# A decoder layer on one core: weight preparation in column blocks, bias rows turned on TensorE

## The reference

```python
qkv = x @ qkv_w.T + qkv_b                 # 256 -> 2048 + 512 + 512
q, k = rope(q), rope(k)
w = exp(logits - m) / (sum(exp(logits - m)) + exp(sink - m))
out = (w @ v) @ out_w.T + out_b           # 2048 -> 256
```

## Time and profile before

| | us |
|---|---|
| median of 3 runs | 1864.81 (1863.73 to 1865.49) |
| profiled execution | 1871.08 |
| its span | 1869.2 |
| TensorE busy in the span | 1731.8 (93%) |
| VectorE, GpSimd, ScalarE busy | 1183.3, 838.4, 811.3 |

### The profile page before, as it was taken

How to read it: one execution, slowest core, us unless ns; L and a number is a source line. 1 busy time by engine, 2 the same in 40 slices (tenths; PEclk the granted TensorE clock), 3 DMA queues, 4 the chain that set the end, 5 groups by cost and what they waited for, 6 DMA issues and landing times. The chain is left out here.

```text
span 1869.2 us, 45277 instructions
## 1 busy us (share of the span) xinstructions
PE 1731.8 (93%) x15345; PEld 1392.1 (74%) x15441; DVE 1183.3 (63%) x2269; ACT 811.3 (43%) x1575; POOL 838.4 (45%) x1302
## 2 busy tenths in 40 slices
PE   3999999999999999999699999999995789999997
PEld 2788888888888888888577777777773788866664
DVE  5777777777777777777478888888782334422221
ACT  2434434433433443343247777777673233311111
POOL 4455655555565465555334444444444211144443
PEclk9999999999999999999789999999997799999999
DMA  5021121112112111111334444444432454222221
GB/s 181 20 58 43 42 56 53 36 51 56 42 42 56 50 36 53 56 39 41 90 95 113 115 117 115 124 126 121 115 101 62 139 208 147 74 63 68 67 64 38
DMA packets 145343, 148.43 MB, mean 79 GB/s; under 512 B 26194, under 2 KB 139926, under 8 KB 143482
## 3 DMA queue, kind: packets, MB, share of 16 engines
q1 hardware_dynamic: 139514, 133.46, 25.6%
q0 software_dynamic: 5760, 14.06, 2.4%
HBM read 93.46 MB, written 54.11 MB: 79 GB/s over the span
## 5 line engine op out<-in xcount | busy, mean ns | idle before, releaser
L1149 DVE TENSOR_REDUCE xmax<-bankX 128x4 f32<-128x1024 f32 x256 | 308.8, 1217 | 63.7 <-PE bankX L1234 58.0
L1102 ACT ACTIVATE xe<-bankXT 128x512 f32<-128x512 f32 x512 | 291.7, 598 | 91.3 <-PE bankXT L1245 75.1
L1245 PE MATMUL bankXT<-stq,stk 98*128 98x256 f32 x1024 | 228.5, 309 | 11.5 <-ACT xe L1102 4.9
L369 POOL TENSOR_TENSOR roped<-ropeC,ropeD 128x512 f32<-128x512 f32 x160 | 205.1, 1290 | 57.8 <-DVE ropeD L530 57.7
L1245 PEld LDWEIGHTS bankXT<-stq,stk 98*128 98x128 f32 x1024 | 155.2, 190 | 53.7 <-ACT xe L1102 31.2
L557 DVE TENSOR_TENSOR oTl<-bankV,oTh 128x512 fp32r<-128x512 f32 x128 | 88.2, 689 | 167.0 <-ACT oTh L445 167.0
L662 PE MATMUL bankQ<-wqh,xnTh 128*128 128x512 f32 x384 | 189.4, 493 | 0.0
L1234 PE MATMUL bankX<-stk,stq 96*128 96x256 f32 x1024 | 172.0, 292 | 14.8 <-DMA rw<-in_rw 10.9
L361 POOL TENSOR_TENSOR prob<-prob,rden 128x1024 f32<-128x1024 f32 x64 | 121.9, 1904 | 88.4 <-DVE rden L553 88.4
L1234 PEld LDWEIGHTS bankX<-stk,stq 96*128 96x128 f32 x1024 | 145.1, 197 | 19.0 <-DMA rw<-in_rw 11.1
L728 PE MATMUL bankO<-woh,oTh 128*128 128x256 f32 x512 | 152.5, 298 | 0.0
(11 more groups left out here) (196 smaller groups left out, 4021.9 us busy)
## 6 DMA issues: line engine op xcount, KB each, us to landing
stackk_d<-chl SPq DMA_DIRECT2D x96, 128.0 KB, 2.3
stackq_d<-q2hl SPq DMA_DIRECT2D x96, 128.0 KB, 2.3
stk<-stackk_d SPq DMA_DIRECT2D x32, 384.0 KB
stq<-stackq_d SPq DMA_DIRECT2D x128, 96.0 KB
wexp<-in_wexp SPq DMA_DIRECT2D x8, 1536.0 KB
x_d<-x SPq DMA_DIRECT2D x64, 128.0 KB, 1.9
xrden<-inv_d SPq DMA_DIRECT2D x64, 128.0 KB, 2.5
xin<-xg_d SPq DMA_DIRECT2D x40, 128.5 KB, 2.1
```

The lines of the kernel that those rows point to most:

```text
L369: nc.gpsimd.tensor_tensor(roped[c % 3][:], ropeC[c % 2][:], ropeD[c % 2][:], ALU.add).then_inc(s_rsum, 1)
L1102: nc.scalar.activation(xe[q][:].rearrange("p n m -> p (n m)"), bT[:, q % 2, :], ACT.Exp).then_inc(s_xe, 1)
L1149: nc.vector.tensor_reduce(xmax[tile[1] % 2][:, :, a:b + 1:b - a].rearrange("p m h -> p h m"), bS[:, 2 * (pr % 2):2 * (pr % 2) + 2, :].rear ...
L1245: ins = nc.tensor.matmul(bT[:, q % 2, n * D:(n + 1) * D], stk[p][0:98, hd // 4, n * P:(n + 1) * P], stq[p][0:98, hd, :], start=True, stop= ...
```

## The change

- The columns of the joint matrix are reordered: keys, values, then queries, and its three blocks are column blocks (both halves of the width, 1,024 columns each). Block 0 serves keys and values, blocks 1 and 2 the queries. TensorE waits for a block's subtraction only ahead of the projection that first uses it.
- Raw blocks live in three slots, so the two output blocks are loaded into slots 0 and 1 after the subtractions of blocks 0 and 1. They are rounded by ScalarE at the end of its tile 0, and subtracted by GpSimd at the end of its tile 0 (`s_loo`), not by VectorE.
- The bias comes as one array of columns; its three terms are turned into rows by 26 small matmuls against the identity, into seven PSUM banks, which ScalarE copies into `bias3`.
- The first x and the bias are loaded ahead of the constants. Tile 0's statistics come first on VectorE; GpSimd clears `bias3` first, and `zeros`, `half` and `vbd` between the two `rsqrt`.

```diff
-            sp.dma_start(const[:], A["const"]).then_inc(s_const, 16)
-            for p in range(2):
-                sp.dma_start(x[p][:], A["x"][p * P:(p + 1) * P, :]).then_inc(s_x[p], 16)
-            sp.dma_start(bcol[:, 0:24], A["bqkv"].rearrange("(p c) -> p c", c=24)).then_inc(s_bias, 16)
-            sp.dma_start(bcol[:, 24:26], A["bo"].rearrange("(p c) -> p c", c=2)).then_inc(s_bias, 16)
+            sp.dma_start(bcol[:], A["bias"]).then_inc(s_bias, 16)
+            sp.dma_start(x[0][:], A["x"][0:P, :]).then_inc(s_x[0], 16)
+            sp.dma_start(const[:], A["const"]).then_inc(s_const, 16)
+            sp.dma_start(x[1][:], A["x"][P:2 * P, :]).then_inc(s_x[1], 16)
             for i in range(NSTAGE):
-                sp.dma_start(stage[:, i, :], wsrc[i]).then_inc(s_stage[i], 16)
+                if i >= 3:
+                    sp.wait_ge(s_lo, i - 2)
+                sp.dma_start(slot[i], wsrc[i]).then_inc(s_stage[i], 16)
...
-            sp.wait_ge(s_bterm, 1)
-            for k in range(3):
-                sp.dma_start(G.bias_d[k, 0:3072].rearrange("(p c) -> p c", c=24), bterm[:, k, 0:24]).then_inc(s_brow, 16)
-                sp.dma_start(G.bias_d[k, 3072:NBIAS].rearrange("(p c) -> p c", c=2), bterm[:, k, 24:26]).then_inc(s_brow, 16)
-            sp.wait_ge(s_brow, 96)
             sp.wait_ge(s_setg, 2)
-            sp.dma_start(bias3[0:3, :], G.bias_d).then_inc(s_brows, 16)
-            sp.wait_ge(s_setg, 1)
...
@@ gpsimd, end of body
+                if isinstance(num(tile), int) and num(tile) == 0:
+                    for n in (3, 4):
+                        pool.wait_ge(s_hi, n + 1)
+                        nc.gpsimd.tensor_tensor(wlo[n], raw[n], whi[n].bitcast(F32), ALU.subtract).then_inc(s_loo, 1)
 
             rsqrt(0, (0, 0))
+            nc.gpsimd.memset(zeros[:, 0:D], 0.0)
+            nc.gpsimd.memset(G.half[:], 0.5)
+            pool.wait_ge(s_const, 16)
+            nc.gpsimd.tensor_copy(zeros[:, D:D + 1].bitcast(I32), C["none"]).then_inc(s_setg, 1)
+            for p in range(2):
+                for b in range(2):
+                    ins = nc.gpsimd.memset(vbd[p][b][:], 0.0)
+            ins.then_inc(s_setg, 1)
             rsqrt(0, (0, 1))
...
@@ scalar
-            for i in range(NSTAGE):
+            for i in range(7):
+                act.wait_ge(s_brow, i + 1)
+                if i == 0:
+                    act.wait_ge(s_setg, 1)
+                a, b = 512 * i, min(512 * i + 512, NBIAS)
+                nc.scalar.activation(bias3[0:3, a:b], BROW[i][0:3, 0:b - a], ACT.Copy).then_inc(s_brows, 1)
+
+            def high(i):
+
                 act.wait_ge(s_stage[i], 16)
-                nc.scalar.activation(whi[i], stage[:, i, :], ACT.Copy).then_inc(s_hi, 1)
+                nc.scalar.activation(whi[i], raw[i], ACT.Copy).then_inc(s_hi, 1)
...
+                if isinstance(num(tile), int) and num(tile) == 0:
+                    high(3)
+                    high(4)
 
             turn_norm((0, 0))
+            for i in range(3):
+                high(i)
             tiles(act, body)
...
@@ vector
                 if front:
                     rope(tile, 0)
+                    if isinstance(t, int) and t == 0:
+                        low(2)
                     if below(t, NT - 1):
                         turn_rest(ahead(tile))
...
-            dve.wait_ge(s_sinks, 16)
             stats1((0, 0))
+            dve.wait_ge(s_const, 16)
+            nc.vector.tensor_copy(identb[:], ident).then_inc(s_setv, 1)
             norm1((0, 0))
+            nc.vector.tensor_copy(maskb[:], C["mask"])
+            nc.vector.tensor_copy(run[:], C["base"]).then_inc(s_setv, 1)
+            low(0)
             turn_rest((0, 0))
             stats1((0, 1))
             norm1((0, 1))
+            low(1)
             tiles(dve, body)
...
@@ tensor, in project
+                if isinstance(t, int) and t == 0 and c in (0, 1, 3):
+                    pe.wait_ge(s_lo, (c + 3) // 2)
...
+            pe.wait_ge(s_setv, 1)
+            pe.wait_ge(s_bterm, 1)
+            for c in range(NBIAS // P):
+                ins = nc.tensor.matmul(BROW[c // 4][0:3, c % 4 * P:(c % 4 + 1) * P], bterm[:, :, c], identb[:],
+                                       start=True, stop=True)
+                if c % 4 == 3 or c == NBIAS // P - 1:
+                    ins.then_inc(s_brow, 1)
             turn_norm((0, 0))
-            pe.wait_ge(s_setv, 1)
-            pe.wait_ge(s_brows, 16)
-            pe.wait_ge(s_lo, NSTAGE)
+            pe.wait_ge(s_setv, 2)
+            pe.wait_ge(s_brows, 7)
             tiles(pe, body)
```

More of the change, by code:

```diff
@@ L176, in attention @@
         NBIAS = 3072 + D
[L177 to L180, removed]
+        stage01 = sb("stage01", [P, 2, 2048])
+        bcol = sb("bcol", [P, NBIAS // P])
+        bterm = sb("bterm", [P, 3, NBIAS // P], BF16)
         ropeC = [sb(f"ropeC{p}", [P, 512]) for p in range(2)]
@@ L185, in attention @@
         kT = sb("kT", [P, NKV // 2, P])
+        with nc.sbuf_tensor("stage2", [P, 2048], F32) as stage2:
+            pass
         prob = sb("prob", [P, 2, 16 * HD + 16])
@@ L192, in attention @@
         s_stage = [sem(f"s_stage{i}") for i in range(NSTAGE)]
-        s_hi, s_lo = sem("s_hi"), sem("s_lo")
+        s_hi, s_lo, s_loo = sem("s_hi"), sem("s_lo"), sem("s_loo")
         s_bias, s_setv, s_setg = sem("s_bias"), sem("s_setv"), sem("s_setg")
@@ L214, in attention @@
         s_q2hl, s_chl, g_c, g_q2 = sem("s_q2hl"), sem("s_chl"), sem("g_c"), sem("g_q2")
-        whi = [wqh[:].rearrange("p k n -> p (k n)")[:, i * 2048:(i + 1) * 2048] for i in range(3)] + [
+        whi = [wqh[:, :, i * 1024:(i + 1) * 1024] for i in range(3)] + [
             woh[:].rearrange("p k n -> p (k n)")[:, i * 2048:(i + 1) * 2048] for i in range(2)]
-        wlo = [wql[:].rearrange("p k n -> p (k n)")[:, i * 2048:(i + 1) * 2048] for i in range(3)] + [
+        wlo = [wql[:, :, i * 1024:(i + 1) * 1024] for i in range(3)] + [
             wol[:].rearrange("p k n -> p (k n)")[:, i * 2048:(i + 1) * 2048] for i in range(2)]
+        slot = [stage01[:, 0, :], stage01[:, 1, :], stage2[:], stage01[:, 0, :], stage01[:, 1, :]]
+        raw = [slot[i].rearrange("p (k n) -> p k n", k=2) for i in range(3)] + slot[3:]
         wsrc = [A["wqkv"][:, i * 2048:(i + 1) * 2048] for i in range(3)] + [
             A["wo"][:, i * 2048:(i + 1) * 2048] for i in range(2)]
-        COL = [NH * HD] + [512 * i for i in range(4)] + [(NH + NKV) * HD]
+        COL = [0] + [1024 + 512 * i for i in range(4)] + [512]
+        BROW = [bk[0][:, 0, :], bk[1][:, 0, :], bT[:, 0, :], bS[:, 0, :], bS[:, 1, :], bP[:, 0, :], bV[:, 0, :]]
         def tiles(eng, body):
@@ L312, in _ @@
         def _(pool):
[L313 to L316, removed]
             nc.gpsimd.memset(half_neg[:], -0.5)
             nc.gpsimd.memset(onesb[:], 1.0)
[L319 to L324, removed]
+            nc.gpsimd.memset(bias3[:], 0.0).then_inc(s_setg, 1)
+            pool.wait_ge(s_setg, 1)
             def settle(tile, c):
@@ L423, in evac_v @@
                 act.wait_ge(s_qkv, num(tile) * 6 + 6)
+                if isinstance(num(tile), int) and num(tile) < 2:
+                    act.wait_ge(s_setg, 3)
                 v = bk[1][:, 0, :].rearrange("p (a o d) -> p o a d", o=2, d=HD)
@@ L486, in _ @@
         def _(dve):
-            dve.wait_ge(s_const, 16)
-            dve.wait_ge(s_setg, 2)
             def settle(tile):
@@ L536, in shift @@
             def shift(u, r, ch):
+                if isinstance(num(u), int) and num(u) == 0 and r == 0:
+                    dve.wait_ge(s_sinks, 16)
                 dve.wait_ge(s_S, num(u) * 2 + r + 1)
@@ L565, in residual, with low @@
                 nc.vector.tensor_tensor(x1[pu][:], xres[pu][:], bO[:, 0, 0:D], ALU.add).then_inc(s_x1, 1)
[L567 to L570, removed]
+            def low(i):
+                dve.wait_ge(s_hi, i + 1)
+                nc.vector.tensor_tensor(wlo[i], raw[i], whi[i].bitcast(F32), ALU.subtract).then_inc(s_lo, 1)
+            dve.wait_ge(s_bias, 16)
             ch = Chain(dve, c_bias, 4, 0)
@@ L576, in _ @@
             ch.end()
[L577 to L580, removed]
             def body(tile, front, rear, prep):
@@ L635, in _ @@
             pe.wait_ge(s_const, 16)
-            pe.wait_ge(s_setg, 2)
+            pe.wait_ge(s_setg, 1)
             def turn(out, src, first=True, final=True):
@@ L719, in project_out @@
                 out = bO[:, 0, 0:D]
+                if isinstance(t, int) and t == 0 and g == 0:
+                    pe.wait_ge(s_loo, 2)
                 if g == 0:
@@ L1768, in __init__ @@
         self.x2_d = dram("x2_d", (NT * P, D))
-        self.bias_d = dram("bias_d", (3, 3072 + D), BF16)
         self.inv_d = dram("inv_d", (2, 2, XD, 2, D))
@@ L1821, in layout @@
     feat = (order[:, None] * HD + np.arange(HD)).reshape(-1)
-    qkv = np.concatenate([feat, np.arange(NH * HD, (NH + 2 * NKV) * HD)])
```

(7 more changed lines are left out.)

## The result

In eleven runs each the kernel before took 1866.34 us (median; 1863.03 to 1874.24) and the changed one 1876.86 (1871.3 to 1882.94); the ratio over all these runs is put at 1.0041 [1.0025, 1.0058], and the two medians alone give 1.0056, inside the same interval. It is slower by more than the 0.2% that I took for the limit of the measurement, and lies outside my range. The profiled execution took 1877.91, with a span of 1876.1.

The account below looks back on a forecast made before the run. TensorE, busy 26.5 of 27.0 us per steady tile, was held at the head by VectorE's weight subtractions and the bias's DRAM trip. 13.7 - 4.1 - 3.15 - 5.5 - 2.6 = -1.65 us, so about 1866.4; range 1859.5 to 1870.

Parts of the forecast that it names:

- the head, at projection 0: Start of the kernel: the first projection starts near 15.3 instead of 29.06, 13.7 us earlier.
- second block, at projection 1: Second normalisation, held by GpSimd's clearing, delays block 1's subtraction; projection 1 starts at 23.7, losing 4.1 us of lead.
- context, at turn 4: End of tile 0: context rows queue behind weights and zero writes, land at 35.9; turn 4 at 39.9, 3.15 us lost.
- output weights, at the keys' turn of tile 1: GpSimd's two subtractions, 9.1 us, precede tile 1's first rope sum; keys turn at 55.05, 5.5 us lost.
- clock, at tile 2: After TensorE's wait in tile 1 the clock halves for 5.2 us; half of it, 2.6 us, is lost.
- the rival with 0.33: Head: bias matmuls cost 0.33 us each instead of 0.15, 4.6 us more, total 1871; chance 0.06.
- The first rival: Second normalisation: VectorE gets in between stk and stq clearings, ends at 18.1, gains 3.3 us, total 1863.1; chance 0.12.
- context early: End of tile 0: context lands at 33.9, 2.05 us less; shares chance 0.10 with the clock being kept.
- the third rival: Tile 1: GpSimd's 13 us idle covers its 9.1 us, tile 1 and clock take nothing; about 1858, chance 0.10.
- sign by which I would have been wrong: Tiles 0 and 1: GpSimd's subtractions ending before 50, or a short second normalisation, would refute the forecast.
- from tile 2 on, tiles of 27.3 us as before: Steady loop: tiles from tile 2 on keep taking 27.3 us, as in the kernel before.

Follow-up runs that it names:

- Experiment 7: The changed kernel with context and x rows issued first, and stk and stq cleared ahead of the second reciprocal root; ratio to the kernel before 0.9985 [0.997, 1.0001].
- Experiment 4: The changed kernel with the first two tiles' context, residual and next x rows issued ahead of output weight blocks and zero writes; ratio to the kernel before 1.0002.
- experiment 11: The changed kernel with output weights rounded by ScalarE between tile 0's copies and subtracted by VectorE, not GpSimd; ratio to the kernel before 1.001 [0.9994, 1.0027].
- Experiment 2: The kernel before with only 32 bytes left free ahead of the rotation's tiles; ratio to the unaltered kernel before 1.0016 [1.0003, 1.0029].
- experiment 6: The changed kernel with 224 bytes left free ahead of the rotation's tiles, putting oTh back to residue 192; ratio to the kernel before 1.0018 [1.0, 1.0036].
- experiments 9 and 10: The kernel before, unchanged, executed twice more; tile 2 started at 76.77 and 73.59 us, against 76.79 in the first profile.

## Why the prediction was wrong

Leads are counted against the profile of before: how much earlier the same row stands in after. The difference from one row to the next is the term.

| term | forecast | measured |
|---|---|---|
| the head, at projection 0 | +13.7 | +14.1 |
| second block, at projection 1 | -4.1 | -3.8 |
| context, at turn 4 | -3.15 | -5.0 |
| output weights, at the keys' turn of tile 1 | -5.5 | -5.9 |
| clock, at tile 2 | -2.6 | -0.6 |
| sum | -1.65 | -1.1 |

**The head: right.** Forecast 15.3 for projection 0, measured 14.92. I had the first normalisation held until 9.3; it wasn't (0.42 us at 6.33), and it made no difference, since TensorE was turning the bias until 8.9 anyway. The bias matmuls took 0.11 us, not 0.15, so the rival with 0.33 is out. Projection 0 came 0.4 us sooner than forecast with that.

**The second block: right.** Normalisation forecast 4.4 at 17.0, measured 4.38 at 16.30; projection 1 forecast 23.7, measured 22.94. Experiment 7 gives the price of this one order of two memsets and a root: 3.96 us at projection 1, 3.4 at tile 2. The first rival ("the port is passed on") is out: VectorE was held over both clearings again, in after and in experiments 4 and 11. The rule of the Trainium skill's page "SBUF — State Buffer", section "SBUF: two separate sides", that one instruction locks the shared pair of ports, doesn't agree with these rows if it is read as a turn for VectorE after each.

**The context: right in kind, too small in size.** Landing forecast 35.9, used at 36.62; turn 4 forecast 39.9, came at 40.99, with a lead that had been 0.8 larger: 5.0 us lost for 3.15. TensorE idled 4.41 us, and it is already here that the granted clock fell to 0.50 (38.0 to 48.2), and not in tile 1: the two turns took 1.11 and 1.09 us each. Experiment 4 took the cause away, and the wait and this fall with it: 5.8 us came back at turn 4, 5.4 at tile 2. The rival "context early" priced a landing 2 us sooner at 2.05; that case didn't come, and no run has it.

**The output weights: right in amount, and not seen as one wait.** GpSimd's pair was forecast from 44.6 to 53.7, and ran from 46.15 to 55.26, 9.11 us against 9.1. It held VectorE too, which I had not put down: 3.65 us for an operation of 16 columns (47.11) that takes 0.18 in experiment 11, where GpSimd has no subtraction; TensorE waited 1.51 behind it. The keys' turn came at 56.55, forecast 55.05. The idle time ahead of it was 1.18 us and not 5.5, since TensorE came late itself; where it comes on time (experiment 4) it is 5.25. So the third rival, that the 13 us of GpSimd's idle time cover this work, is refuted. That the order in the queue decides is argued: experiment 11 gives the work to another engine, and no run leaves it to GpSimd behind the rope sums.

**The clock: in another place, and longer.** The level was down for 10.2 us and not 5.2, behind the wait for the context; there was no fall behind GpSimd's work in this kernel. So its cost lies in the two terms ahead of it, and little is left for its own. That a part of it only shortened the wait for GpSimd that came next is argued from the chain; no run separates it. The context's term was 1.9 us too small and the clock's 2.0 too large, and they cancel. That the sum to tile 2 came out at -1.1 is luck in that part. Neither sign by which I would have been wrong came: the subtractions ended at 55.26, the second normalisation was long.

**The step that failed is the last: "from tile 2 on, tiles of 27.3 us as before".** I costed at nothing what the edits of the allocation do, and never asked what they do: `bcol` and `bterm`, 260 B that used to be overlaid, now keep their room, and some 31 steady tiles ((923.35 - 77.90) / 27.4) take 27.433 us instead of 27.333. This is 3.1 us. The attention ended at 923.35 against 919.38, 4.0 late: the 1.1 of tile 2 and 2.9 more. Experiment 2 shows this term by itself in the kernel before, experiment 6 takes it out of after. It stood in no rival of mine. With it out (experiment 6) the ratio is 1.0018 [1.0, 1.0036], and my forecast, 1.65 of 1865 us or 1.0009, lies inside.

**A second size was off: the row the sum went against.** It was one execution, and experiments 9 and 10 put the mean of three at 75.7 instead of 76.79. The two make 2.3 + 3.1 = 5.4 us, a ratio of 1.0029, within both intervals ([1.0025, 1.0058] and [1.0019, 1.0046]). The difference to the first ratio, 1.0041, is 2.2 us, to the second, 1.0033, 0.8. I have no cause shown for it. From the attention's end to the end of the span the three executions of before took 949.8, 953.8 and 951.6 us (for instance 1869.2 - 919.38), and the two of after 952.7 and 948.2: no loss of the later stages can be told from this, and they differ by more than the 2.2 between executions of one kernel.

In absolute terms the miss is 10.5 us (1876.86 for 1866.4). Of these 1.5 are the base: the median of before is 1866.34 in eleven runs and was 1864.81 in the three that I had. The place is 3.1, and tile 2, 2.3 late for 1.65, is 0.65. The other 5.2 have no cause shown; 2.9 of them are only the distance of the two medians, 10.5, from the 7.7 us that the ratio 1.0041 stands for. The range was narrow as well: two of my own rivals, 1858 and 1871, lay outside the 1859.5 to 1870 given for all.

**What stays open.** Why the place costs. The experiments move a whole group of tiles (`prob`, `roped` and the others too), so they don't show that it is the pair `oTh` and `woh` in whose reads the 2 to 3 ns arise, though the groups that slow most are those that read them. Against it stand the projections: their operands don't move, and in after and in experiment 2 their rows on `wqh` are 0.3 to 0.4 us longer all the same (170.3 for 170.0; 137.4 for 137.0). A run with only this pair moved was not made. Nor is the removal of the DRAM trip separate from the blocks' order here: no run has one without the other.

## What to carry to other kernels

When an edit changes what is allocated, work out where the tiles behind it move, and compare the mean duration of the steady loop's groups first: 2 to 3 ns on each of 48 matmuls are 0.1 us a tile and 3.1 us in all, as much as I had put the wait for the context at. A gain at the head lasts only if all that was hidden behind the old wait moves along: its DMA issues, and the work of a shared queue. And a single row of one execution is no firm base for a sum whose result is a tenth of a per cent; look at two more executions of the unchanged kernel before.

## What was not expected of the hardware

- 32 B of SBUF placement change the mean of a 128x256 matmul from 279 to 282 ns and a tile from 27.333 to 27.433 us; weights, `xnTh` and `oTh` at a multiple of 256 give 27.381, a distance of 128 between `oTh` and `woh` gives 27.379.
- VectorE is held over several GpSimd instructions in a row (4.38 us over two clearings; 3.65 us over GpSimd's first subtraction for a 16-column operation), and yet one normalisation got through within 0.42 us at 6.33, beside a clearing of 256 columns. GpSimd is held by VectorE too: 4.54 us for two rope sums that take 2.48 alone.
- In the attention the granted clock fell to 0.50, the 1.2 GHz level, behind waits of TensorE of 4.41 us (after), 5.25 (experiment 4, where the window from 50.0 to 53.5 reads 0.52, and experiment 7, where 44.2 to 50.9 reads 0.50) and 3.33. The waits of 1.51 and 1.18 us in after's tile 1, in the window 45.6 to 77.9, brought none: the 512-column bias matmul behind the second took 0.38 us. It stayed down for 10.2, some 3.4, 6.8 and 10.2 us, so my 5.2 stood between them.
